# One cross-attention step re-ordered across steps, its scores split into 64-row tiles, its output accumulated with query rows on partitions

## The reference, cut to what matters

```python
# ctx_1024: (1, 25088, 512); x: (1, 256, 512); wi: (512, 64); Wo: (1024, 512)
qp = layernorm(x) @ wi ; kp = ctx @ wi ; vp = ctx @ wi      # keys and values are the same rows
attn = softmax(qp @ kp.T / 8)
head = qp + attn @ vp
x = x + tile(head, 16) @ Wo + bo
```

## Time and profile before

| | us |
|---|---|
| median of three timed runs | 647.61 (647.19 to 650.44) |
| span of the profiled execution | 645.2 |
| the 21 steps from 50.02 to 285.92 | 235.9 |
| from 285.92 to 309.30 (rest of the last step, product with Wo) | 23.4 |
| from 309.30 to the end | 335.9 |

### The profile page before, as it was taken

The page is one execution under the profiler, slowest core; times in us unless marked ns, Lnnn a source line. Parts: engine busy times, 40 slices in busy tenths (PEclk is TensorE's granted clock), DMA queues, the critical chain, the costliest instruction groups (busy, mean ns, idle before and its releaser), DMA issues.

```text
span 645.2 us, 8980 instructions
## 1 busy us (share of the span) xinstructions
PE 580.2 (90%) x3085; PEld 383.0 (59%) x3085; DVE 463.5 (72%) x762; ACT 374.4 (58%) x631; POOL 20.3 (3%) x38
## 2 busy tenths in 40 slices
PE   4879999999999999998699568799859999999995
PEld 2334545454554545454379447677657888888883
DVE  2486666666666666665777885779888899898994
ACT  2525464555546354554166675368738788887882
POOL 2060000000000000000000000000000000000000
PEclk9989999999999999998699779999969999999999
DMA  8854646556574838400525301112966989788100
GB/s 327 301 195 165 252 174 244 206 216 239 180 276 142 313 130 297 158 1 0 196 106 175 112 1 66 66 54 101 372 256 225 360 314 331 279 321 320 66 1 35
DMA packets 34059, 122.12 MB, mean 189 GB/s; under 512 B 2545, under 2 KB 2545, under 8 KB 29426
## 3 DMA queue, kind: packets, MB, share of 16 engines
q1 hardware_dynamic: 31858, 113.93, 47.7%
q0 software_dynamic: 1904, 7.34, 3.0%
q10 hardware_dynamic: 272, 0.52, 0.2%
HBM read 121.26 MB, written 0.52 MB: 189 GB/s over the span
## 4 chain that ended last, share of the span: by engine, by line
PE 80%; DVE 10%; ACT 6%; issue 2%; DMA 1%; SPq 0%; DVEq 0%; ACTq 0%
PE bank L417 14%; PE score_banks L856 13%; PE bank L433 10%; PE bank L490 9%; PE bank L889 7%; PE score_banks L427 5%; PE score_banks L428 4%; PE score_banks L572 3%; PE score_banks L618 2%; PE bank L474 2%; PE score_banks L816 1%; PE score_banks L713 1%; PE score_banks L737 1%; DVE w_split L1519 1%; ACT arena L1064 1%
## 5 line engine op out<-in xcount | busy, mean ns | idle before, releaser
L1392 DVE TENSOR_TENSOR w_split<-arena,w_split 128x1024 fp32r<-128x1024 f32 x96 | 114.3, 1221 | 6.6 <-ACT w_split L1019 4.4
L1019 ACT ACTIVATE w_split<-arena 128x1024 fp32r<-128x1024 f32 x96 | 100.8, 1060 | 14.8 <-PE score_banks L856 10.5
L417 PE MATMUL bank<-arena,wi_sb 128*64 128x512 f32 (+1 forms) x400 | 91.4, 600 | 8.2 <-DMA arena<-in_ctxT 8.2
L856 PE MATMUL score_banks<-w_split,xg 128*128 128x512 f32 x384 | 88.7, 390 | 1.4 <-ACT xg L1184 1.4
L1276 DVE TENSOR_REDUCE small<-score_banks 128x1 f32<-128x1024 f32 (+1 forms) x50 | 60.1, 1203 | 34.1 <-PE score_banks L428 34.1
L856 PEld LDWEIGHTS score_banks<-w_split,xg 128*128 128x128 f32 x384 | 71.8, 188 | 17.0 <-ACT xg L1184 1.7
L490 PE MATMUL bank<-probsT,kv 128*64 128x256 f32 x392 | 65.0, 410 | 3.8 <-DVE probsT L1269 3.6
L433 PEld LDWEIGHTS bank<-ident,probs 128*128 128x128 f32 x392 | 41.8, 141 | 41.1 <-issue 36.7
L926 ACT ACTIVATE kv<-bank 128x512 f32<-128x512 f32 (+1 forms) x25 | 14.7, 588 | 87.1 <-PE bank L433 87.1
L433 PE MATMUL bank<-ident,probs 128*128 128x128 f32 x392 | 59.3, 285 | 2.0 <-ACT probs L939 2.0
L1269 DVE COPY probsT<-bank 128x512 f32<-128x512 f32 x49 | 33.9, 691 | 37.8 <-PE bank L433 37.8
(11 more groups left out here) (249 smaller groups left out, 847.6 us busy)
## 6 DMA issues: line engine op xcount, KB each, us to landing
arena<-in_ctxT SPq DMA_DIRECT2D x24, 2048.0 KB, 7.6
arena<-in_w12T SPq DMA_DIRECT2D x32, 1024.0 KB, 6.3
arena<-in_w3T SPq DMA_DIRECT2D x16, 1024.0 KB, 6.0
arena<-in_fKT SPq DMA_DIRECT2D x4, 1024.0 KB, 7.2
arena<-in_fV SPq DMA_DIRECT2D x4, 1024.0 KB, 5.3
arena<-in_Wo SPq DMA_DIRECT2D x1, 2048.0 KB, 16.4
arena<-in_ctxT SPq DMA_DIRECT2D x1, 1024.0 KB, 6.8
arena<-in_kKT POOLq DMA_DIRECT2D x1, 1024.0 KB, 10.2
```

Source lines behind the costliest of these rows:

```text
L417: last = pe.matmul(kp_bank[DH * h:DH * (h + 1), 0:half], wi_sb[:, k, :], ctx_buf[:, b, k, h * half:(h + 1) * half], start=(k == 0), stop=( ...
L856: last = pe.matmul(SB[2 * half + h], lhs[:, k, :], w[:, part, 512 * h:512 * (h + 1)], start=(k == 0 and n == 0), stop=(k == KC - 1 and n = ...
L1019: act.activation(w_split[:, i % 4, 0, :], raw, ACT.Copy).then_inc(part_high, 1)
L1392: return dve.tensor_tensor(w_split[:, i % 4, 1, :], raw, w_split[:, i % 4, 0, :].bitcast(F32), ALU.subtract)
```

## The change

A step still holds two halves of 512 context rows. What changes is which step's work stands next to which, how scores are formed, and how the output is kept.

```diff
-        k_split = w_split[:, 0, 0, :].rearrange("p (h n) -> p h n", h=2)
+        k_hi, k_lo = w_split[:, 0, 0, 0:HALF], w_split[:, 0, 0, HALF:2 * HALF]
+        acc = o_acc[:].rearrange("p (s c) -> p s c", s=ST)
+        v_flat = [kv[:, 1, :], hT[:, 0:2, :].rearrange("p k t -> p (k t)")]      # values of two steps
+        o_sb, acc_T = hT[:, 2, :], hT[:, 3, :]
-        diag = sb("diag", [P, ST, P])
-        fade = tiny(ST)
+        fade = [tiny(ST), tiny(ST)]
-        wo_sum, wo_dup, bo_row = arena[:, 7, 0:C], arena[:, 7, C:2 * C], arena[0:1, 7, 2 * C:3 * C]
+        wo_ext, bo_row = arena[0:DH + 1, 7, 2 * C:3 * C], arena[DH:DH + 1, 7, 2 * C:3 * C]
@@ POOL
+            pool.memset(q_full[:], 1.0).then_inc(ev("q_one_done"), 1)
@@ PE
+            def turn_keys(s, half):
+                pe.wait_ge(k_full_done, s + 1)
+                pe.wait_ge(k_lo_done, s + 1)
+                for j in range(half // P):
+                    last = pe.transpose(kp_bank[:, j * P:(j + 1) * P], k_full[:, j * P:(j + 1) * P], ident[:])
+                last.then_inc(keys_turned, 1)
+            def scores(s, half, before=None):
+                for st in range(ST):
+                    if st and before is not None:
+                        pe.wait_ge(probsT_dve, before)
+                        pe.wait_ge(probsT_act, before)
+                    for n, (q, k) in enumerate(((q_hi, k_hi), (q_hi, k_lo), (q_lo, k_hi))):
+                        for h in range(2):
+                            rows = slice(DH * h, DH * (h + 1))
+                            last = pe.matmul(score_banks[:, 2 * st + h, 0:half], q[rows, st * P:(st + 1) * P], k[rows, 0:half],
+                                             start=(n == 0), stop=(n == 2))
+                    last.then_inc(scores_ready, 1)
+            turned_bank = [score_banks[:, 2, :], score_banks[:, 3, :], turn_bank[0], turn_bank[1]]
+            def turn_probs(s, half):
+                pe.wait_ge(probs_ready, 2 * s + 2)
+                for g in range(half // P):
+                    for h in range(2):
+                        for st in range(ST):
+                            c = ST * h + st
+                            last = pe.transpose(turned_bank[g][:, c * P:(c + 1) * P],
+                                                probs[:, st, h * half + g * P:h * half + (g + 1) * P], ident[:])
+                    last.then_inc(probs_turned, 1)
+            def turn_o(s):
+                pe.wait_ge(o_out, s + 1)
+                for st in range(ST):
+                    last = pe.transpose(of_bank[:, T + st * P:T + (st + 1) * P], o_sb[:, st * P:(st + 1) * P], ident[:])
+                last.then_inc(o_turned, 1)
+            def pv(s, b, half, turned_out, added=None):
+                pe.wait_ge(probsT_dve, turned_out)
+                pe.wait_ge(probsT_act, turned_out)
+                pe.wait_ge(v_done, s + 1)
+                if added is not None:
+                    pe.wait_ge(o_added, added)
...
+            def next_keys(s, b):
+                pe.wait_ge(ctx_in[b], 8 * s + (16 if b == 0 else 8))
+                pe.wait_ge(v_done, s)
+                kp(s, b, HALF)
+            def step(s, b):
+                turn_probs(s - 1, HALF)
+                turn_o(s - 2)
+                turn_keys(s, HALF)
+                scores(s, HALF, before=2 * s - 2)
+            def rest_of_step(s, b):
+                pv(s - 1, 1 - b, HALF, 2 * s - 1, s - 1)
+                next_keys(s + 1, 1 - b)
...
+            step(LAST - 2, 0)
+            pe.matmul(turn_bank[0], fold[:], wo_sum, start=True, stop=True).then_inc(ev("wo_folded"), 1)
+            rest_of_step(LAST - 2, 0)
+            step(LAST - 1, 1)
+            rest_of_step(LAST - 1, 1)
+            step(LAST, 0)
+            pv(LAST - 1, 1, HALF, 2 * LAST - 1, LAST - 1)
+            pe.wait_ge(probs_ready, 2 * LAST + 1)
+            for st in range(ST):
+                pe.matmul(SB[st], q_full[0:DH + 1, st * P:(st + 1) * P], wo_ext, start=True,
+                          stop=True).then_inc(ev("xattn_ready"), 1)
+            turn_o(LAST - 1)
+            turn_probs(LAST, HALF)
+            pe.wait_ge(ev("acc_faded"), 1)
+            for st in range(ST):
+                last = pe.transpose(kp_bank[:, st * P:(st + 1) * P], acc[:, st, :], ident[:])
+            pv(LAST, 0, HALF, 2 * LAST + 1, LAST)
+            pe.wait_ge(ev("o_total"), 1)
+            for st in range(ST):
+                pe.matmul(SB[2 + st], o_sb[:, st * P:(st + 1) * P], wo_dup, start=True, stop=True).then_inc(ev("xattn_ready"), 1)
@@ ACT
+            def keys_out(s, half):
+                act.wait_ge(kp_done, s + 1)
+                act.activation(k_full[:, 0:half], kp_bank[:, 0:half], ACT.Copy).then_inc(k_full_done, 1)
+                act.activation(k_hi[:, 0:half], kp_bank[:, 0:half], ACT.Copy).then_inc(k_hi_done, 1)
...
+            def o_copy(s):
+                act.wait_ge(o_ready, s + 1)
+                act.activation(o_sb, of_bank[:, 0:T], ACT.Copy).then_inc(o_out, 1)
+            def step(s, b):
+                keys_out(s, HALF)
+                probs_out(1, 4 * s - 4)
+                probs_out(3, 4 * s - 2)
+                values_out(s, b, HALF)
+                soft(s, b, HALF)
+                o_copy(s - 1)
@@ DVE
+            def k_low(s, half):
+                dve.wait_ge(k_hi_done, s + 1)
+                dve.tensor_tensor(k_lo[:, 0:half], k_full[:, 0:half], k_hi[:, 0:half].bitcast(F32),
...
+            def add_o(s, b, first=False):
+                dve.wait_ge(o_turned, s + 1)
+                turned_o = of_bank[:, T:2 * T].rearrange("p (s c) -> p s c", s=ST)
...
+                    for st in range(ST):
+                        last = dve.scalar_tensor_tensor(out=acc[:, st, :], in0=acc[:, st, :], scalar=fade[b][:, st:st + 1],
+                                                        in1=turned_o[:, st, :], op0=ALU.mult, op1=ALU.add)
+            def step(s, b, first_o=False):
+                probs_out(0, 4 * s - 5)
+                k_low(s, HALF)
+                probs_out(2, 4 * s - 3)
+                add_sums(s - 1, 1 - b)
+                add_o(s - 2, b, first=first_o)
+                maxima(s, b, HALF)
+                delta(s, b)
```

More of the change, by code:

```diff
@@ L419, in kp @@
                 last.then_inc(kp_done, 1)
[L421 to L437, removed]
-                nt = half // P
[L439 to L488, removed]
@@ L497, in step @@
[L497 to L506, removed]
+                last.then_inc(o_ready, 1)
+            def next_keys(s, b):
+                pe.wait_ge(ctx_in[b], 8 * s + (16 if b == 0 else 8))
+                pe.wait_ge(v_done, s)
+                kp(s, b, HALF)
@@ L528, in _ @@
             last.then_inc(ev("q_ready"), 1)
+            turn_keys(0, HALF0)
             pe.wait_ge(ev("q_high"), 1)
             pe.wait_ge(ev("q_split"), 2)
[L531 to L535, removed]
+            scores(0, HALF0)
+            next_keys(1, 1)
+            turn_probs(0, HALF0)
+            turn_keys(1, HALF)
+            scores(1, HALF, before=1)
@@ L916, in _, with probs_out, values_out, soft @@
         def _(act):
[L917 to L922, removed]
-                act.activation(k_full[:, 0:half], kp_bank[:, 0:half], ACT.Copy).then_inc(k_full_done, 1)
[L925 to L934, removed]
+            def keys_out(s, half):
+                act.wait_ge(kp_done, s + 1)
+                act.activation(k_full[:, 0:half], kp_bank[:, 0:half], ACT.Copy).then_inc(k_full_done, 1)
+                act.activation(k_hi[:, 0:half], kp_bank[:, 0:half], ACT.Copy).then_inc(k_hi_done, 1)
+            turned_bank = [score_banks[:, 2, :], score_banks[:, 3, :], turn_bank[0], turn_bank[1]]
+            def probs_out(g, count):
+                act.wait_ge(probs_turned, count)
+                act.activation(probsT[:, g, :], turned_bank[g], ACT.Copy).then_inc(probsT_act, 1)
+            def values_out(s, b, half):
+                act.wait_ge(keys_turned, s + 1)
+                act.activation(v_flat[b][:, 0:half], kp_bank[:, 0:half], ACT.Copy).then_inc(v_done, 1)
+            def soft(s, b, half, first=False):
                 if not first:
@@ L1281, in maxima, with add_sums @@
                                           ALU.min).then_inc(max_ready, 1)
-            def fade_diagonal(s):
-                dve.wait_ge(fade_ready, s)
-                for st in range(ST):
-                    dve.tensor_scalar(diag[:, st, :], ident[:], fade[:, st:st + 1], None, ALU.mult).then_inc(diag_ready, 1)
-            def step(s, b, first=False, next_half=HALF):
-                half = HALF0 if first else HALF
-                nt = half // P
-                slot = 0 if first else b
-                u = 0 if first else 5 * s - 2
-                dve.wait_ge(turned, u + 2)
-                turn_out((slot + 1) % 2, probsT[:, 0, :])
-                if next_half:
-                    k_low(0, s + 1, next_half)
-                if nt == 4:
-                    dve.wait_ge(turned, u + 4)
```

(8 more changed lines are left out.)

147 lines of the change are left out of this document (82 added, 65 removed).

## The result

The changed kernel takes **604.26 us** (four runs, 601.27 to 607.32) where the kernel before takes 648.13 (647.19 to 650.44): a ratio of 0.931, 95% interval 0.928 to 0.934. The forecast was 604.0, 594 to 632. The profiled execution has a span of 602.2 us and took 604.05.

A forecast was written before the change was run, and what follows sets the result against it. PE's own time was taken to bound the cross-attention: 248.7 through step 23 plus 17.0 for the end is 265.7 against 309.30, 43.6 less; span 601.6 plus 2.4 gives 604 us, range 594 to 632.

The forecast's parts named there:

- PE's sum: PE's pieces in one new cross-attention step: 9.4 us, 9.55 with one wait, 9.58 used; gain 1.65 a step.
- Row tiles side by side: Score matmuls on two 64-row tiles run two for the price of one: six pairs at 0.24, 1.4 us a step.
- rivals 1 to 3: Scores: tiles take turns (635), loads show (629), together 0.16 in full; or each tile change costs 0.15 (676), 0.05.
- The wait for the low keys: Before the key transposes, PE waits for the low part of the step's own keys: 0.1 to 0.2 us.
- The other engines: In the step, DVE, ACT and DMA stay covered: probabilities 1.5 us early, `o_added` tightest, DMA load 0.68.
- The start: First steps: PE reaches step 2 about 31.2, and probabilities are next turned from 46.5 us, between 44 and 49.
- The POOL stretch: Near the start, POOL's additions still hold DVE's low part and small sums, with a PE gap of about 4 us.
- The end: From the start of step 24: 15.5 us at full clock plus 1.5 for the clock, 17.0; before, 23.38.
- The part left alone: Everything behind the cross-attention, with nothing in it changed: stays at 335.9 us.
- The rule weighed: For score matmuls, whether weight loads overlap only with matmuls of another row group; the forecast sided with the trace, against this.
- rival 2: In the scores, the next pair's weight load shows: +1.1 a step, 629 us; chance 0.16 together with rival 1 in full.

The follow-up runs named there:

- the experiment: Changed kernel with the key transposes moved between the score tiles of the first and second query rows: 606.77 us against 604.98.
- the halves in turn: Changed kernel with each query tile's score matmuls issued three for half 0, then three for half 1: 605.78 us against 604.98.

## Why the prediction was right, point by point

**PE's sum.** Right, and for the reasons given: 9.4 forecast without the wait and 9.46 measured where none shows, 0.15 forecast for the wait and 0.13 measured, 9.58 and 9.59 together. `pv`, projection and scores came as priced (1.88 with its shape change, 3.43, 1.59). A shape change costs 0.17 by the experiment (0.34 for two), 0.15 to 0.20 by the differences between pieces (0.59 and 0.44 for key transposes, 0.43 and 0.23 for a first score matmul). The sum's 0.45 for three was 0.48: what is left of 9.46 after 2.42, 1.41, 1.72 and 3.43.

**Row tiles side by side.** Right, by the run with extra matmuls; rivals 1 to 3 fell, since six pairs in 1.59 leave no room for loads that show. My later picture of it, in the expectation for the halves in turn, was too narrow: I had taken alternation of the halves to be needed, and it is not.

**The wait for the low keys.** Right in place and size (0.13 of 0.1 to 0.2), and it needn't be there.

**The other engines.** Right. `o_added` was ready by 184.1 with `pv` starting at 184.96; the maxima began at 184.38, behind the scores and not behind DVE's additions; slack 1.9 for 1.5. DMA share 0.65 for 0.68.

**The start.** Right in its sum for this profile, and that is luck: step 3 begins at 46.44 where 46.5 was forecast, but at 47.97 in the same kernel's second profile. PE reached step 2 at 29.96, not 31.2, and at 31.04 in the second profile; the difference is there already when step 1 begins, at 21.25 in one and at 22.32 in the other. So 31.2 was not wrong, and why a run is 1.1 earlier there stays open. The POOL stretch was wrong: it cost 16.48 and 16.93, and not 15.3. I had counted DVE's holds but not that PE, after 4.35 of idling, works at 1.2 GHz for a while, a granted clock of 0.79 and 0.80 over the step (with the halves in turn it was 0.89, and the step 15.39):

```profile
31.27 5.08 DVE L1276 TENSOR_TENSOR w_split<-kv,w_split 128x512 fp32r<-128x512 f32 x1
31.28 4.52 POOL L380 TENSOR_TENSOR arena<-arena 128x2048 f32<-128x2048 f32 x1
...
36.50 1.09 PE L413 MATMUL bank<-ident,kv 128*128 128x128 f32 x4 [4.35 <-DVE w_split L1276]
...
37.52 2.93 PE L425 MATMUL score_banks<-w_split,hidT 64*128 64x512 f32 x12
```

Twelve score matmuls take 2.93 here and 1.66 elsewhere.

**The end.** 14.86 where I had 17.0, of which 1.5 was for the clock. It wasn't needed: the longest idle of PE before the final product is 0.57, the granted clock is 1.00 in that stretch, where before it was 0.89 after a wait of 2.02:

```profile
260.08 1.95 PE L458 MATMUL bank<-probsT,kv 128*64 128x256 f32 x16 [0.52 <-DVE probsT L1283]
...
262.60 1.98 PE L545 MATMUL score_banks<-arena,hT 128*128 128x512 f32 x4 [0.57 <-DVE hT L1375]
...
263.76 0.75 DVE L1401 SCALAR_TENSOR_TENSOR xres<-score_banks,small,xres 128x512 f32<-128x512 f32 x1
```

**The part left alone.** Forecast 335.9, measured 338.44 in this profile. It is in no instruction of the change: from the first key score on, 327.68 before and 330.2 here, and 327.2 to 331.3 over all profiles. The error of 2.5 took the place of the 2.1 that the end gained, so that the time came within 0.3 of the forecast is luck; the mechanism and the gain per step are not.

**The rule weighed.** That a weight load overlaps only with matmuls of another row group (the Trainium skill, "TensorE: Matmul & The Clock Gate", "Part 3: Packing small matmuls — row/col tiling") made rival 2. The runs side against it: consecutive terms of one row tile follow at 0.23 a pair, with loads of 0.18 to 0.19 each.

## What to carry to other kernels

Where PE is busy in every slice, read the starts of its pieces and count changes of tile shape: joining pieces of one shape gave 1.1 (0.44 + 0.31 + 0.15 + 0.20) of the 1.65 a step here, more than the cheaper score matmuls did (0.46). When steps are interleaved so that PE never waits, the smallest helper between two of its pieces becomes the bound, and each wait should name the last reader that really matters: moving one semaphore gave 0.13 a step. And look for the one stretch that doesn't repeat: three additions on POOL cost 5.8 to 7.3 us (a step of 15.39 to 16.93 for one of 9.59), and DVE could do them in its idle time.

## What the runs showed of the hardware that I had not expected

- Matmuls on two 64-row tiles ran two at a time although the program issued three for one tile and then three for the other (1.60 for 12, against 1.59 alternating), and with three extra ones for the lower tile, one of the upper tile started ahead of them. The Trainium skill says in "TensorE: Matmul & The Clock Gate" ("Part 3: Packing small matmuls — row/col tiling") that matmuls start and end strictly in program order; these runs do not agree with that for a stream on two row tiles.
- A POOL addition of 128x2048 kept a DVE subtraction between SBUF tiles waiting for its whole 4.52 us (0.69 became 5.08), and this addition and two smaller ones (128x1024 and 128x512) turned a step of 9.6 into one of 16.5.
- The same instructions behind the cross-attention took 327.2 to 331.3 us in twelve profiles, as the spells at 1.2 GHz fell.
